# One attention and LoRA block on one core: three reorderings of GpSimd's work, and batch 2's finish moved to VectorE ahead of batch 3's last additions

## What is computed

```python
sa, ca, ga, sb, cb, gb = mod(c)                    # from silu(c) @ wmod; |ga|, |gb| at least 0.25
h = layernorm(x) * (1 + ca) + sa
x = x + ga * attention(h)                          # 16 heads of 128; q, k, v, o weights = codes * scales
h = layernorm(x) * (1 + cb) + sb
x = x + gb * (h @ W.T + lora(h))                   # top 2 of 8 experts, rank 16, weights from a softmax
```

## Time and profile before

| | |
|---|---|
| median of 3 runs | 760.81 us (760.44 to 762.17) |
| profiled execution, time | 760.71 us |
| profiled execution, span | 758.9 us |
| mean granted TensorE clock | 0.998 |
| busy: PE, DVE, POOL, ACT | 750.8, 648.5, 627.4, 567.0 us |

### The profile page before, as it was taken

One profiled execution on the slowest core, in us unless ns is written; L12 is line 12 of the kernel. 1 busy time (PEld: TensorE's weight loads), 2 busy tenths in 40 slices (PEclk: granted clock), 3 DMA queues, 4 the chain that ended last, 5 costly groups with the idle time before them and its releaser, 6 DMA issues.

```text
span 758.9 us, 15088 instructions
## 1 busy us (share of the span) xinstructions
PE 750.8 (99%) x4128; PEld 650.4 (86%) x4128; DVE 648.5 (85%) x1263; ACT 567.0 (75%) x1230; POOL 627.4 (83%) x657
## 2 busy tenths in 40 slices
PE   8999999999999999999999999999999999999998
PEld 7888888878888888888888888888888888888887
DVE  7899989889798888879798888979798788889766
ACT  4788787877777777777778787777778787778751
POOL 4587999899798888979888788979888788989962
PEclk9999999999999999999999999999999999999999
DMA  8354334553355344543455344553455345645202
GB/s 261 92 154 126 92 97 125 134 130 94 95 148 155 97 103 121 157 131 93 102 148 156 94 105 125 149 131 93 102 148 152 98 104 146 160 126 144 59 1 111
DMA packets 71725, 92.19 MB, mean 121 GB/s; under 512 B 19477, under 2 KB 36598, under 8 KB 71670
## 3 DMA queue, kind: packets, MB, share of 16 engines
q1 hardware_dynamic: 52368, 73.21, 37.6%
q10 hardware_dynamic: 19302, 18.42, 8.1%
HBM read 23.39 MB, written 2.11 MB: 34 GB/s over the span
## 4 chain that ended last, share of the span: by engine, by line
PE 93%; POOL 2%; DVE 2%; ACT 1%; issue 1%; DMA 0%; SPq 0%; POOLq 0%; ACTq 0%
PE score L1640 15%; PE score L1641 15%; PE score L1642 15%; PE o L1640 7%; PE o L1641 7%; PE o L1642 7%; PE qv L1640 3%; PE qv L1641 3%; PE qv L1642 3%; PE ky L1640 3%; PE ky L1641 3%; PE ky L1642 3%; PE y L1912 2%; PE y L1908 2%; PE y L1907 2%
## 5 line engine op out<-in xcount | busy, mean ns | idle before, releaser
L595 POOL TENSOR_TENSOR pT_parts<-pT,pT_hi 128x512 fp32r<-128x512 f32 x224 | 285.1, 1297 | 55.4 <-ACT pT_hi L852 53.1
L921 ACT ACTIVATE prob<-score,neg_max 128x512 f32<-128x512 f32 x256 | 173.1, 687 | 69.9 <-DVE neg_max L1405 69.8
L1420 DVE STREAM_TRANSPOSE pB<-prob 128x512 f32<-128x512 f32 x252 | 161.5, 686 | 15.6 <-PE o L1642 11.1
L1405 DVE TENSOR_REDUCE neg_max<-score 128x1 f32<-128x512 f32 x256 | 159.1, 679 | 0.5 <-PE score L1642 0.2
L852 ACT ACTIVATE pT_hi<-pT 128x512 fp32r<-128x512 f32 x224 | 129.8, 623 | 3.4 <-DMA pT<-pB 2.5
L1640 PE MATMUL score<-k_hi,q_hi 128*128 128x512 f32 x256 | 101.2, 395 | 0.3 <-DVE q_lo L1292 0.2
L1641 PE MATMUL score<-k_lo,q_hi 128*128 128x512 f32 x256 | 100.4, 392 | 0.0
L1642 PE MATMUL score<-k_hi,q_lo 128*128 128x512 f32 x256 | 99.8, 390 | 0.0
L1640 PE MATMUL o<-pT_hi,v_hi 128*128 128x512 f32 x248 | 97.0, 391 | 0.1
L1641 PE MATMUL o<-pT_parts,v_hi 128*128 128x512 f32 x248 | 96.5, 389 | 0.0
L1642 PE MATMUL o<-pT_hi,v_lo 128*128 128x512 f32 x248 | 96.5, 389 | 0.0
(11 more groups left out here) (466 smaller groups left out, 2039.4 us busy)
## 6 DMA issues: line engine op xcount, KB each, us to landing
pT<-pB SPq DMA_DIRECT2D x1008, 64.0 KB, 2.0
x_nat<-in_L_attn_x_dram ACTq DMA_DIRECT2D x4, 512.0 KB, 4.6
out_dram<-x_nat SPq DMA_DIRECT2D x8, 256.0 KB, 2.0
stage<-in_L_attn_wv_codes_dram ACTq DMA_DIRECT2D x7, 256.0 KB
stage<-in_L_attn_wv_scales_dram ACTq DMA_DIRECT2D x14, 128.0 KB
stage<-in_L_attn_wq_codes_dram ACTq DMA_DIRECT2D x7, 256.0 KB
stage<-in_L_attn_wq_scales_dram ACTq DMA_DIRECT2D x14, 128.0 KB
stage<-in_L_attn_wk_codes_dram ACTq DMA_DIRECT2D x7, 256.0 KB
```

The lines of the kernel that those rows point to most:

```text
L595: pool.tensor_tensor(turned_quarter(par, i, pT_lo), turned_quarter(par, i), quarter(pT_hi, i).bitcast(f32), ALU.subtract).then_inc(p_lo_ok, 1)
L921: act.activation(prob[:, i], score_ps[i][:, :], ACT.Exp, bias=neg_max[:, i:i + 1], accum_out=row_sum[:, s % 2, i:i + 1]).then_inc(exp_ok, 1)
L1405: dve.tensor_reduce(neg_max[:, i:i + 1], score_ps[i][:, :], AX.X, ALU.max, negate=True).then_inc(max_ok, 1)
L1420: dve.transpose(pB[:, s % 2, :, :, i].rearrange("p g k q -> p k g q"), prob[:, i].rearrange("p (k g q) -> p k g q", k=QT, g=G)).then_inc(p ...
```

## The change

It has three places.

1. Start: POOL waits for both of DVE's `input_lo` (`h_lo` at 2) before `parts("q", 0, 1)`.
2. Pair 1, POOL alone: `input_mix_lo(1, 4)` goes ahead of `block_sums("q", 2)`; both `parts_1` go from the end of step 4 to step 5, behind `mixed_low`; `parts_s23("q", 2)` goes behind `mixed_low` in step 6. All are still ahead of that step's `prob_low`.
3. Tail: DVE, not POOL, makes `gate(2)` and `attended(2)`, and with `statistics(2)` they go ahead of `y_add(N-2)` and `y_add(N-1)`. ACT makes `lora_out(1)` ahead of `ffn_normalise(2)`. PE makes the first of two tiles of `dense(2, 0)` ahead of `ffn_input(3)`.

```diff
             parts("q", 0, 0)
+            pool.wait_ge(h_lo, DC)
             parts("q", 0, 1)
...
+            def parts_1_ahead(p):
+                pool.wait_ge(k_mm, SPP + 2 * cycle(p, 1) + 1)
+                parts_1("q", p + 1)
+                parts_1("k", p + 1)
+
+            def s23_ahead(p):
+                pool.wait_ge(product_mm["k"], products(7, cycle(p, 1) + 1))
+                parts_s23("q", p + 1)
...
                         if isinstance(p, int) and p == 1:
                             input_mix_lo(1, 3)
+                            input_mix_lo(1, 4)
                         block_sums("q", p + 1)
-                        if isinstance(p, int) and p == 1:
-                            input_mix_lo(1, 4)
                         block_sums("k", p + 1)
...
                     elif s == 6:
-                        pool.wait_ge(product_mm["k"], products(7, cycle(p, 1) + 1))
-                        parts_s23("q", p + 1)
+                        if not (isinstance(p, int) and p == 1):
+                            s23_ahead(p)
...
                             mixed_low(m, u3 if s % 4 == 1 else u2, mixed)
+                    if isinstance(p, int) and p == 1 and s == 5:
+                        parts_1_ahead(p)
+                    if isinstance(p, int) and p == 1 and s == 6:
+                        s23_ahead(p)
...
-                    if s == 4 and not last:
-                        pool.wait_ge(k_mm, SPP + 2 * cycle(p, 1) + 1)
-                        parts_1("q", p + 1)
-                        parts_1("k", p + 1)
+                    if s == 4 and not last and not (isinstance(p, int) and p == 1):
+                        parts_1_ahead(p)
...
             times_gb(1)
-            gate(2)
-            attended(2)
             times_gb(2)
...
             ffn_input_high(1)
+            lora_out(1)
             ffn_normalise(2)
-            lora_out(1)
             ffn_input_high(2)
...
             o_low(N, to=(q_hi, q_lo))
+            gate(2)
+            attended(2)
+            statistics(2)
             y_add(N - 2, B - 1, 3, False)
             dve.wait_ge(y_ok, QT * (N - 1))
             y_add(N - 1, B - 1, 2, False, y_end)
-            dve.wait_ge(x1_ok, 3)
-            statistics(2)
             gate(B - 1)
...
             lora_rows(2)
+            pe.wait_ge(y_ok, QT * N)
+            dense(2, 0, (0,))
             ffn_input(3)
-            pe.wait_ge(y_ok, QT * N)
-            dense(2, 0)
+            dense(2, 0, (1,))
             lora_rows(3)
```

## The result

The changed kernel's median is 763.41 us (761.94 to 763.51) where the kernel before gives 760.81 us (760.44 to 762.17) beside it, over seven runs of each. The ratio is 1.0023, 95% interval 1.0014 to 1.0032: slower, by 1.1 to 2.4 us. The forecast was 762.3 us, its range 760.9 to 763.2. By the ratio the changed kernel takes 762.6 us where the one before takes 760.81, which is in the range; the plain median lies 0.2 us above it. The prediction had put 0.45 on "slower by over 0.2%", where the ratio just lies, and 0.50 on a difference within 0.2%. Four executions far off all others (821.7 to 1925.95 us, one with the kernel before and three with experiments) are left out of the ratios.

A forecast was written before the change was run, and what follows sets the result against it. TensorE was taken to bound the kernel, never resting from 280 to 715 us, so earlier stalls reach the end whole. Start 0, pair 1 +0.35 and tail +1.2 gave +1.55 us: 762.3 us, range 760.9 to 763.2.

The forecast's parts named there:

- Start, 0: At the start, POOL's new wait costs and wins nothing, since no row shows TensorE waiting there: 0 us.
- the 0.14 of the bounds: At the start, the largest gain allowed, if all time from 13.52 to 13.66 were a wait that goes: 0.14 us.
- Pair 1, +0.35: Steps 4 to 7: product 4's 0.91 us is given back, and POOL idles 0.37 awaiting `q_hi` before `mixed_low`: +0.35 us.
- weighted(13) at 188.0 "from the start": Sign for pair 1, step 7: `weighted` starts at about 188.0 us instead of 187.63; before 187.6 would refute POOL holding it.
- Tail, batch 2: In the tail, TensorE's 0.92 us wait ahead of `ffn_input(2)` goes, with `ffn_normalise(2)` ending at 730.6, before 731.20.
- Tail, batch 3: In the tail, VectorE's added work delays statistics to 734.1, `ffn_input(3)` to 738.25 and `lora_rows(3)` to 740.4 (+0.9 us).
- Tail, the router, +1.2 at the end: In the tail, `router(0)` starts 1.2 us later, at 738.5, and the end moves with it: +1.2, bounds +0.9 and +1.5.
- TensorE's own +0.9: In the tail, `lora_rows(3)` starts at 740.4 instead of 739.54; the router is later still.
- Rival 1: In the tail, batch 2's gain is kept and the kernel is not slower: 760.3 us; chance 0.09.
- Rival 3: In the tail, TensorE's clock falls after its waits near 737 and 740: 763.3 to 764 us; chance 0.07.
- Rival 2: Pair 1 costs nothing and the tail is milder (+0.4 to +1.2): 761.2 to 762.0 us; chance 0.24.
- The sum: Whole kernel: start 0, pair 1 +0.35 and tail +1.2 make +1.55 us, a time of 762.3 us.

The follow-up runs named there:

- start_alone: Kernel before with only the change's start wait added; ratio 0.9998 [0.9988, 1.0009].
- pool_alone: Kernel before with only the change's pair 1 reorderings on POOL; ratio 1.0004 [0.9996, 1.0013], pair 1 stretch 31.02 us against 30.74.
- mix_alone: Kernel before with only `input_mix_lo(1, 4)` moved ahead of `block_sums` of q; ratio 1.0003 [0.9994, 1.0012], pair 1 stretch 30.79 us against 30.74.
- act_order: Kernel before with only ACT's `lora_out(1)` ahead of `ffn_normalise(2)`; ratio 0.9995 [0.9985, 1.0006], tail 35.14 us against 35.51.
- tail_gate3_quarter: tail_alone with VectorE's gate of batch 3 cut to one tile of four, leaving computation out; ratio 1.0011 [0.9998, 1.0024], tail 35.85 us.
- tail_lora2: tail_alone with ACT making `lora_out(2)` ahead of `ffn_normalise(3)`; ratio 1.0013 [1.0003, 1.0024] to the kernel before, tail 36.41 us.
- late_parts: mix_alone's edit, plus pair 1's `parts_1` behind step 5's `prob_low` and `parts_s23("q")` in step 7; ratio 0.9993 [0.9984, 1.0003], pair 1 30.23 us.
- best_split: best_late, but q's weights stay in step 4 and only k's move behind step 5's `prob_low`; median 760.11 us, ratio 0.9987 [0.9977, 0.9997] to before.
- tail_alone: Kernel before with only the change's tail edits (POOL, ACT, VectorE, TensorE); ratio 1.0011 [1.0001, 1.0020], tail 36.65 us against 35.51.
- best_late: Kernel before with the edits of late_parts and act_order together; median 760.02 us beside 760.88, ratio 0.9992 [0.9983, 1.0002].

## Why the prediction was right, point by point

- **Start, 0.** Right for executions whose clock falls there: start_alone's stretches are those of before. The reasoning took TensorE's times from rows at a clock of 0.50; at 1.00 TensorE waits for both halves, and the wait looks to be worth 0.2 to 0.4 us, more than the 0.14 of the bounds. The second subtraction got quicker (2.12 to 1.70 us for the two) and the first did not. The trace agrees with the Trainium skill ("SBUF — State Buffer", Who interferes with whom): the first subtraction starts 0.24 us after `wq_lo` of 0.79 and is still held up by it until it ends, since the pair takes 1.70 us (1.10 and 0.68, overlapping by 0.08) and not the 1.3 to 1.4 of two such instructions undisturbed (0.68 to 0.69 us each elsewhere in the trace). By the other reading, a shared port, the two would have ended up to 0.2 us earlier as an estimate.
- **Pair 1, +0.35.** Right in size and in mechanism: +0.32 in the changed kernel, +0.28 in pool_alone. mix_alone shows the first half (0.9 won at product 4, 0 kept) and the timeline the second. `q_hi` was done 12.81 us after `input_mix_lo(1, 3)`, where 170.69 - 156.89 = 13.80 before: 0.99 earlier, not 0.91, so POOL's idle time was 0.26 by the starts, not 0.37; the remaining 0.05 is small growth in POOL's own instructions.
- **weighted(13) at 188.0 "from the start".** Wrong as a time from the start: it came at 187.43, and by the prediction's own test, "before 187.6, so that POOL didn't hold it", this would have spoken against the mechanism. The test was badly put: it took the start for fixed, and this execution's start was 0.52 us shorter. From the nearest anchor it was 0.32 later, with POOL's row as its releaser.
- **Tail, batch 2.** Right: the wait of 0.92 is gone, `ffn_normalise(2)` ended at 730.16, before 731.00. Wrong in part as to what it needed: act_order gets 0.37 of it with the order of two ScalarE steps alone.
- **Tail, batch 3.** Right to 0.3 us in each row: statistics done at 733.88 (forecast 734.1), `ffn_normalise(3)` at 735.43 (735.7), `ffn_input(3)` at 737.99 (738.25), `lora_rows(3)` at 740.16 (740.4). Most of these differences are one: this tail began 0.20 us earlier than before's (720.02 for 720.22). tail_gate3_quarter shows that VectorE's queue holds the end one for one.
- **Tail, the router, +1.2 at the end.** The size was right (+1.12), the term that carried it was not quite. I had the router's +1.2 as what decides and TensorE's own +0.9 behind it. tail_lora2 takes the router's delay away, and still has +0.90 of the +1.14: TensorE's chain from `ffn_input(3)` carries 0.9, and the router 0.24 on top. The two terms were sized rightly; they nearly tie, and only one of them could be cured by reordering ScalarE.
- **The rivals.** Rival 1 (batch 2's gain is kept) failed where the prediction had it decide: VectorE's 2.54 us met 1.1 us of slack. Rival 3 (the clock falls) didn't happen: TensorE waited 1.67 us and, at 740, another 0.40, and the granted clock from 715 to 755 us is 1.00; a tile of four still takes 0.87 (748.84 to 749.71). Rival 2 had its first half wrong, pair 1 does cost.
- **The sum.** +1.55 forecast, +1.44 by the two stretches, +1.0 by the ratios of the three parts run alone (1.0011, 1.0004 and 0.9998), and 1.0023 [1.0014, 1.0032] for the whole, which is +1.1 to +2.4. The median difference of 2.60 us rests on seven runs of each; the forecast's +1.55 is inside the ratio's interval, and no stretch of this one trace holds a further microsecond. Spans of equal mean clock differ by 1.6, so most of the rest seems to be which executions the two medians fell on; no run shows that for certain.

## What to carry to other kernels

All of this is from one kernel. Ahead of every reordering, find the engine that is late at the next meeting point and count its work up to there: moving that engine's work about within the stretch wins nothing (mix_alone), moving it past the meeting point wins, but only as far as what is left fills the engine's waits (late_parts against best_split). An engine without idle time is no place for work that another one had time for: here 2.54 us more for VectorE bought 0.9 us at one wait and gave back 2.0 behind it, while the free half, one swap on an engine that was waiting, won 0.37. Where the start scatters by more than the effect, cut both traces at common instructions, and write tests of a forecast as distances from such an anchor, not as times from the start.

## What I had not expected of the hardware

**The start isn't the same twice.** The first score began at 17.95 us in before's profiled execution and 17.43 in after's, and between 16.88 and 19.37 over all profiled kernels, ten of which have the very same start. In part it goes with the granted clock of TensorE between 12 and 20 us: where it was 1.00 throughout (four profiles), the first score came at 16.88 to 17.79 us, with about 3 us at 0.50 (seven) at 17.78 to 18.47, and with nearly 7 us at 0.50 (one) at 19.37. Stretches of before, of after and of tail_gate3_quarter, in this order:

```profile
12.00:14.00 2.00, 2.00 (x8) 1.59 (x7) 1.97 (x3) 1.44 (x5) 1.91 (x3) 0.50 1.11 213
14.00:16.00 2.00, 2.00 (x13) 2.00 (x13) 1.75 (x8) 0.20 (x1) 1.16 (x2) 0.68 1.06 314
```

```profile
12.00:14.00 2.00, 0.98 (x7) 0.67 (x6) 1.97 (x3) 1.28 (x5) 1.09 (x2) 1.00 1.10 244
14.00:16.00 2.00, 2.00 (x18) 2.00 (x19) 1.93 (x9) 0.73 (x2) 1.42 (x3) 1.00 1.06 273
```

```profile
12.00:14.00 2.00, 1.32 (x6) 0.81 (x5) 1.97 (x4) 1.26 (x5) 1.92 (x3) 0.54 1.08 260
14.00:16.00 2.00, 1.98 (x9) 2.00 (x10) 1.93 (x7) 0.00 (x0) 1.40 (x2) 0.50 1.11 326
16.00:18.00 2.00, 2.00 (x12) 2.00 (x11) 1.14 (x3) 0.95 (x2) 1.37 (x3) 0.50 0.81 285
18.00:20.00 2.00, 2.00 (x12) 1.87 (x12) 1.22 (x3) 1.12 (x3) 0.10 (x1) 0.75 0.24 98
```

The clock stays at its high level (2.4 GHz) in after, falls to the low one (1.2 GHz) for about 3 us in before and for nearly 7 in tail_gate3_quarter. after idled more in 12 to 14 us (PE busy 0.98) than before did (2.00, drawn out by the low clock) and kept its clock. What decides it in an execution these runs don't show; that the clock can stay up without the change is shown by tail_alone, which has before's start and kept 1.00 as well (16.88). It isn't the only scatter, for in 34 executions of before, beside the first experiments, the time exceeds the span by anything from 1.76 to 3.68 us; both are reasons why an effect of 0.3 us needs a stretch and not a median.

**VectorE ends 0.55 us after the POOL instruction that was there first, and the delays add up.** In mix_alone, 60 us ahead of its edit, TensorE waited 0.81 us by the starts, up to 97.55, for VectorE's `k_lo`. VectorE was 2.4 us later there than in before, counted from the first score, and three instructions had made it so: `x_nat<-u,x_nat` at 74.66 took 1.65 us (0.97 in before), and then these two, 0.68 each in before:

```profile
84.31 5.96 POOL L602 TENSOR_TENSOR pT_parts<-pT,pT_hi 128x512 fp32r<-128x512 f32 x4 [0.49 <-ACT pT_hi L962]
86.00 1.42 DVE L1322 TENSOR_TENSOR x_nat<-u,x_nat 128x512 f32<-128x512 f32 x1
87.34 1.78 DVE L1322 TENSOR_TENSOR z<-router_space,y_acc 128x512 f32<-128x512 f32 x1
```

All three began while one of POOL's 128x512 instructions was running (0.19, 0.44 and 0.52 us after its start), and all three ended 0.55 us after it. So did every VectorE `TENSOR_TENSOR` of 128x512 that took over 0.8 us in the profiles of before, mix_alone and best_late, 19 in all, the start's subtractions among them. best_late had the same pair of delays (1.56 and 1.77 us), and a wait of TensorE behind it at 96.63. That these delays made TensorE's waits is read from the traces, and no run tested it; with them first score to `weighted(13)` took 170.38 us in mix_alone's profile and 169.68 in before's, though pair 1 was level. The loop has such scatter too: `weighted(13)` to the last out-projection took between 532.59 and 533.67 us over the profiled kernels, with no edit in it.
